# Cross attention on one core: where Q's six passes stand in TensorE's sub-step

## The reference

```
qh = heads(x @ wq.T + bq);  kh = heads(ctx @ wk.T + bk);  vh = heads(ctx @ wv.T + bv)
scores = qh @ kh.T / sqrt(32)  + mask * (-2**32 + 1)      # (512 x 77) for each head
attn   = softmax(scores) ;  out = merge(attn @ vh) + x
out    = (out - mean(out)) / sqrt(var(out) + 1e-5) * gamma + beta
```

## Time and profile before

| | us |
|---|---|
| median of three runs | 1106.25 |
| the profiled execution's own time | 1106.21 |
| its span, first to last instruction | 1104.4 |
| TensorE busy | 1072.8 (97%) |
| VectorE busy | 935.7 (85%) |
| GpSimd busy | 775.4 (70%) |
| ScalarE busy | 723.0 (65%) |

### The profile page before, as it was taken

How to read it: one execution, slowest core, us unless ns; L and a number is a source line. 1 busy time by engine, 2 the same in 40 slices (tenths; PEclk the granted TensorE clock), 3 DMA queues, 4 the chain that set the end, 5 groups by cost and what they waited for, 6 DMA issues and landing times.

```text
span 1104.4 us, 26985 instructions
## 1 busy us (share of the span) xinstructions
PE 1072.8 (97%) x7549; PEld 984.7 (89%) x7549; DVE 935.7 (85%) x1784; ACT 723.0 (65%) x1140; POOL 775.4 (70%) x682
## 2 busy tenths in 40 slices
PE   7999889999999999999999999999999999999985
PEld 7888779999999999999999999999999999999984
DVE  6988578888888888888888888888898888888876
ACT  3321366777777777777777777777777777777653
POOL 4999713676777777777777677777777777777568
PEclk9999999999999999999999999999999999999988
DMA  7754644565565566555556665565666555554452
GB/s 227 256 169 178 206 110 116 135 165 150 148 165 151 156 165 165 152 144 151 142 145 161 164 163 144 150 166 149 158 164 165 146 147 150 143 144 127 127 156 86
DMA packets 176906, 171.34 MB, mean 155 GB/s; under 512 B 110004, under 2 KB 111556, under 8 KB 176868
## 3 DMA queue, kind: packets, MB, share of 16 engines
q1 hardware_dynamic: 167044, 145.36, 46.1%
q10 hardware_dynamic: 9824, 25.50, 10.1%
HBM read 96.76 MB, written 48.85 MB: 132 GB/s over the span
## 4 chain that ended last, share of the span: by engine, by line
PE 91%; DVE 3%; POOL 2%; ACT 1%; issue 1%; DMA 1%; POOLq 0%; ACTq 0%; SPq 0%; DVEq 0%
PE q_ps L863 31%; PE o_ps L935 24%; PE t_ps L897 12%; PE s_ps L883 11%; PE v_ps L608 4%; PE s_ps L886 3%; PE q_ps L567 2%; PE k_ps L567 2%; DVE row_max L1069 1%; POOL k_part L303 1%; POOL y L1154 1%; DMA q_b<-q_b 1%; PE k_ps L624 1%; POOL y L1157 0%; DVE probs L1078 0%
## 5 line engine op out<-in xcount | busy, mean ns | idle before, releaser
L935 PE MATMUL o_ps<-v_tiles,pt 128*128 128x66 f32 x2500 | 309.2, 271 | 0.2 <-DVE attn L989 0.2
L935 PEld LDWEIGHTS o_ps<-v_tiles,pt 128*128 128x128 f32 x2500 | 300.9, 193 | 0.9 <-issue 0.9
L1264 ACT COPY pt<-t_ps 128x512 f32<-128x512 f32 x316 | 184.2, 583 | 157.5 <-PE t_ps L897 154.5
L1069 DVE TENSOR_REDUCE row_max<-s_ps 128x8 f32<-128x616 f32 x256 | 204.7, 800 | 97.3 <-PE s_ps L886 86.1
L1177 POOL TENSOR_TENSOR x_lo<-xT_raw,x_hi 128x512 fp32r<-128x512 f32 x120 | 153.1, 1276 | 188.0 <-ACT x_hi L1236 188.0
L1226 ACT ACTIVATE probs<-probs 128x616 f32<-128x616 f32 x256 | 184.2, 720 | 83.5 <-DVE probs L1078 77.7
L863 PE MATMUL q_ps<-x_lo,wq_hi 128*128 128x512 f32 x496 | 221.9, 447 | 0.0
L1144 POOL TENSOR_TENSOR attn<-attn,x_rows 128x512 f32<-128x512 f32 x124 | 159.1, 1283 | 86.2 <-DVE attn L989 86.2
L1078 DVE TENSOR_TENSOR probs<-s_ps,row_max 128x616 f32<-128x616 f32 x256 | 204.7, 799 | 5.7
L897 PE MATMUL t_ps<-ident,probs 128*128 128x128 f32 x1260 | 193.0, 276 | 4.2 <-ACT pt L1264 2.3
L863 PE MATMUL q_ps<-x_hi,wq_lo 128*128 128x512 f32 x496 | 195.8, 395 | 0.0
(11 more groups left out here) (130 smaller groups left out, 1694.0 us busy)
## 6 DMA issues: line engine op xcount, KB each, us to landing
xT_raw<-in_xT SPq DMA_DIRECT2D x128, 256.0 KB, 3.3
out<-y SPq DMA_DIRECT2D x128, 256.0 KB, 2.8
x_rows<-in_x SPq DMA_DIRECT2D x31, 1024.0 KB, 6.2
k_scratch<-k_out SPq DMA_DIRECT2D x8, 1232.0 KB, 5.1
k_ac<-k_scratch SPq DMA_DIRECT2D x256, 38.5 KB, 5.5
q_a<-q_a ACTq DMA_DIRECT2D x64, 128.0 KB, 3.4
q_c<-q_a ACTq DMA_DIRECT2D x64, 128.0 KB, 3.8
q_b<-q_b ACTq DMA_DIRECT2D x64, 128.0 KB, 4.0
```

Source lines behind the costliest of these rows:

```text
L935: mm = pe.matmul(bank_of(b, t)[:, col:col + tile_cols[i]], pt[h][0:w, i, P * t:P * t + P], v_tiles[v_buffer(b, h)][0:w, i, 0:tile_cols[i]] ...
L1069: dve.tensor_reduce(row_max[:, u, :].rearrange("p (j h) -> p j h", j=2), score_heads(t), AX.X, ALU.max).then_inc(max_ready, 1)
L1264: act.copy(pt[h][0:w, i, :], bank[0:w, :]).then_inc(pt_ready, 1)
```

## The change

TensorE's order in a sub-step becomes scores, turns of `TURNS_AHEAD`, Q, product. `TURNS_AHEAD` now holds turns 0, 1, 2, 4 at t = 0, 1, 2, 3, and `TURNS_BETWEEN` holds turn 3 at t = 2, between the first and the last three of Q's passes. On ScalarE the exponent comes first in a sub-step, then the copies of `TURNS_AHEAD`, and the copy of `TURNS_BETWEEN` stands where the copies of `TURNS_BEHIND` stood. No instruction is added or taken away, and the waits of each function stay as they are.

```diff
-            TURNS_AHEAD = ([], [], [2], [])
-            TURNS_BEHIND = ([0], [1], [3], [4])
+            TURNS_AHEAD = ([0], [1], [2], [4])
+            TURNS_BETWEEN = ([], [], [3], [])
...
                         ahead, g, part = q_of_step(s)
-                        between = [(a - 1 + h, 1 - h, i) for i in TURNS_AHEAD[t]] if real(a - 1 + h) else []
+                        if real(a):
+                            scores(a, h, t, par)
+                        if real(a - 1 + h):
+                            for i in TURNS_AHEAD[t]:
+                                turn(a - 1 + h, 1 - h, i)
+                        between = [(a - 1 + h, 1 - h, i) for i in TURNS_BETWEEN[t]] if real(a - 1 + h) else []
                         if real(a + ahead) and not in_phase_one(a + ahead):
                             q_half(a + ahead, g, part, (par + ahead) % 2, between)
                             between = []
                         for i in between:
                             turn(*i)
-                        if real(a):
-                            scores(a, h, t, par)
-                        if real(a - 1 + h):
-                            for i in TURNS_BEHIND[t]:
-                                turn(a - 1 + h, 1 - h, i)
                         if real(a - 1):
                             product(a - 1, h, t)
...
                         h, t = s // 4, s % 4
-                        if real(a - 1 + h):
-                            for i in TURNS_AHEAD[t]:
-                                copy_pt(a - 1 + h, 1 - h, i)
                         if s == 0 and isinstance(a, int) and a == 0:
 
                             high_q(0, NG - 1)
...
                         elif real(a):
                             exponent(a, (s - 1) // 4, (s - 1) % 4)
+                        if real(a - 1 + h):
+                            for i in TURNS_AHEAD[t]:
+                                copy_pt(a - 1 + h, 1 - h, i)
...
                             high_q(a + ahead, g)
                         if real(a - 1 + h):
-                            for i in TURNS_BEHIND[t]:
+                            for i in TURNS_BETWEEN[t]:
                                 copy_pt(a - 1 + h, 1 - h, i)
                         if high and g % 2 == 1:
                             move_q(a + ahead, g // 2)
```

## The result

The changed kernel takes 1373.7 us (1367.84 to 1376.09, 4 runs) against 1105.96 of the kernel before (median of 4 runs beside it): a ratio of 1.2415, 95% interval 1.2395 to 1.2434. The direction and the two waits were forecast. The time lies outside the range of 1235 to 1305, 1.7 us from the price of the rival "the clock falls too", which had a chance of 0.07.

A forecast was written before the change was run, and what follows sets the result against it. TensorE, busy without a wait from 200 to 1040 us, was taken to bound the kernel. 1106.2 + 39.1 (turn 0) + 120.2 (turn 3) + 0.3 (lead-in) + 1 (tail) = 1266.8, so 1267 us; range 1235 to 1305.

The forecast's parts named there:

- the two waits: TensorE waits at turn 0 (0.63 us, 62 times) and at turn 3 in the split (1.97 us, 61 times).
- the clock falls too: Rival: each of 61 long waits also lowers TensorE's clock, losing 1.7 us each, 105 in all: 1372 us; chance 0.07.
- TensorE's own work: New seams between kinds of matmul cancel, Q to product taken as 0; -20 to +20 us kept for the range.
- Chain one: Turn 0 (s = 0 and 4): exponent of tile 3 stands behind Q's pair; wait 0.63 us, 62 times, 39.1 us.
- Chain two: Turn 3 (s = 2 and 6): DMA issues, exponent and copy delay it; wait 1.97 us, 61 times, 120.2 us.
- Lead-in and tail: Element 0's three longer waits replace two of today, +0.3 us; last element's scores of s = 4 come later, +1 us.

The follow-up runs named there:

- the best here: Changed kernel with the DMAs of Q's moves behind the copy of turn 2 and the exponent of row tile 3 ahead of Q's pair: 1163.72 us.
- the last experiment: Kernel before, with 14 passes ahead of the first scores and 13 ahead of the last element's scores of s = 4: 1105.23 us, ratio 1.0009.

## Why the prediction was wrong

- **TensorE's own work costs nothing: right.** It is 3.59 us per sub-step before and after; Q to product, the seam that was not in the trace, is free.
- **Chain one: the mechanism right, the size low.** Forecast was 0.63, measured 0.78 on average and 0.85 in the sub-step shown. There the pair starts 0.28 after the product and not 0.20 (606.99 against 606.71), exponent to turn is 0.86 and not 0.77, and the passes behind the turn come 0.05 later. The average adds 9 us to the 39.1.
- **Chain two: right.** Forecast was 1.97, measured 2.09. The issues hold ScalarE up, as the earlier trace rows had it, and the experiment that moves them shows it. It adds 7 us to the 120.2.
- **Lead-in and tail: small, as forecast.** The chains alone give 1106.2 + 176 = 1282; the kernel with the wait filled, whose clock did not fall, took 1285.4, inside the range. That leaves some 3 us where 1.3 were forecast.
- **The step that failed is the clock.** The prediction kept the granted clock at 1.00, because the lead-in's waits of 1.37 and 1.39 had left it there. That row was read rightly, and experiments with waits of that size agree (idle 1.1 us, no fall). But it was used for waits half a microsecond longer, between these and the wait of 3.42 us behind which the clock had fallen at 136 us, and no row of the trace bore that out; the chance of 0.07 should have been several times that. What the runs showed in its place: the clock fell behind 36 of 57 such waits, and with the wait filled 88 us of the loss were gone. The rival's 1372 came close by luck, two errors that cancel: it had a fall behind each of the 61 waits at 1.7 us, while there are about 40 longer ones, 88 us against 105; and the waits cost 19 more than forecast (1285.4 against 1266.8).
- The Trainium skill (TensorE: Matmul & The Clock Gate, section "HAM oscillation — how this bites in real kernels") tells of a kernel whose waits of some 3 to 5 us between bursts sent the clock to its low level behind every one. This trace agrees in kind, with shorter waits: 1.85 to 1.92 us of idle time and 36 falls behind 57 waits. It differs in that not every wait did it: 8 of 57 in one kernel with such a wait in every half step and 41 of 56 in another.

Left open is why a wait of 1.9 us lets the clock fall at one time and not at another. The runs show that the idle time at turn 0 does not decide it, and they point to the length of the step; they do not show the rule. That some order of the new kind could reach the kernel before is not shown either: the best here is 1163.7 us, with VectorE behind.

## What to carry to other kernels

When a producer is moved closer to a wait, follow the in-order engine between the two through every instruction that stands there, DMA issues among them: here they were the longest piece (1.9 us) of a chain of 4.7 us. Where a new wait is longer than any that the trace shows with a steady clock, price the clock as a forecast and not as a remote rival, and where no shorter chain is to be had, passes that fill the wait can be worth more than they cost. Raising an engine's low clock is worth something only where the end waits for that engine; the last experiment gained nothing by it.

## What the runs showed of the hardware

- The granted clock fell to 1.2 GHz behind many waits with 1.85 us of idle time and more, for 3.4 to 6.8 us. It did not behind waits with 1.1 (half steps of 16.9 us) or 1.2 (half steps of 17.5 us). A half step lengthened from 17.15 to 17.7 us by busy passes took the share of waits with a fall from 8 of 57 to 41 of 56.
- Filling an idle time of 1.9 us with seven passes kept the clock at 1.00 and made the kernel 88 us faster than the changed one, still 180 us slower than the kernel before.
- Three DMA issues in a row on ScalarE keep the next instruction, one that waits for no DMA, from starting for 1.9 us.
